# Other job orders on four engines, and other counts of constant products on TensorE, in a fused two-layer transformer kernel

## The reference, cut to what matters

```
x = x + L0_xattn(layernorm(x), ctx)   # 16 heads of width 8, softmax over 77 keys
x = x + L0_ffn(layernorm(x))          # 128 -> 352 -> 128, SiLU gate; activations and weights rounded to
                                      # 8-bit integers with ONE scale, the maximum over the whole tensor
x = x + L1_xattn(layernorm(x), ctx)   # as the first, with a mask
x = x + L1_ffn(layernorm(x))          # 8 experts of 128 -> 256 -> 128, all computed and summed,
                                      # times a normalised top-1 gate
```

## Time and profile before

| | |
|---|---|
| median of 3 runs | 358.16 us (358.93, 352.06, 358.16) |
| the profiled execution | 357.13 us, its span 355.3 us |
| mean granted TensorE clock over the span | 0.897 of 2.4 GHz |
| PE / DVE / ACT / POOL busy | 82% / 73% / 43% / 30% |
| experts, 251 to 351 us | PE busy 98.70 of 100 us |

### The profile page before, as it was taken

One profiled execution on the slowest core, in us unless ns is written; L12 is line 12 of the kernel. 1 busy time (PEld: TensorE's weight loads), 2 busy tenths in 40 slices (PEclk: granted clock), 3 DMA queues, 4 the chain that ended last, 5 costly groups with the idle time before them and its releaser, 6 DMA issues.

```text
span 355.3 us, 4665 instructions
## 1 busy us (share of the span) xinstructions
PE 290.0 (82%) x1368; PEld 180.3 (51%) x1368; DVE 259.4 (73%) x717; ACT 154.3 (43%) x252; POOL 105.0 (30%) x119
## 2 busy tenths in 40 slices
PE   8594887788886363449778989989999999999995
PEld 3262433444444221223455354624678888888883
DVE  4868368878384489883877377772799998898883
ACT  1110255455663175241025355647734554554541
POOL 5785602001001499021108001010136611603400
PEclk9986599999999857696756599999999999999998
DMA  8558131300005900302223121000000000000000
GB/s 153 168 153 202 45 74 22 83 17 2 8 0 95 241 3 0 118 0 63 64 53 72 27 52 44 9 0 9 2 2 0 0 31 1 0 31 0 1 30 30
DMA packets 12298, 16.92 MB, mean 48 GB/s; under 512 B 3672, under 2 KB 6712, under 8 KB 12265
## 3 DMA queue, kind: packets, MB, share of 16 engines
q1 hardware_dynamic: 10018, 11.75, 14.0%
q0 software_dynamic: 1856, 4.27, 4.6%
q10 hardware_dynamic: 400, 0.61, 0.7%
HBM read 4.90 MB, written 1.05 MB: 17 GB/s over the span
## 4 chain that ended last, share of the span: by engine, by line
PE 45%; DVE 16%; ACT 4%; issue 3%; POOL 1%; DMA 1%; SPq 0%; DVEq 0%; POOLq 0%; ACTq 0%
PE ps_acc L1118 4%; PE ps_acc L1117 4%; PE ps_acc L1116 4%; PE ps_tok L986 4%; PE ps_key L995 3%; PE ps_acc L1144 3%; DVE mx L676 3%; PE ps_key L1103 2%; PE ps_key L902 2%; DVE axb L888 2%; PE ps_key L1104 2%; PE ps_key L1105 2%; PE ps_tok L1103 2%; PE ps_tok L1105 2%; PE ps_tok L1104 2%
## 5 line engine op out<-in xcount | busy, mean ns | idle before, releaser
L676 DVE TENSOR_REDUCE mx<-ps_tok 128x4 f32<-128x312 f32 x128 | 57.2, 476 | 23.4 <-PE ps_tok L986 22.1
L467 ACT ACTIVATE big<-ps_key 117x512 f32<-117x512 f32 (+1 forms) x96 | 53.7, 594 | 42.7 <-PE ps_key L995 41.8
L986 PE MATMUL ps_tok<-kst,qst 97*128 97x312 f32 x128 | 50.7, 433 | 17.2 <-DVE mx L676 11.6
L350 POOL TENSOR_SCALAR veps<-mv 128x4 f32<-128x4 f32 x16 | 4.3, 271 | 157.3 <-DVE mv L584 157.2
L986 PEld LDWEIGHTS ps_tok<-kst,qst 97*128 97x128 f32 x128 | 27.5, 219 | 42.3 <-DVE mx L676 20.7
L825 DVE TENSOR_TENSOR qst<-big,qst 128x512 fp32r<-128x512 f32 x64 | 44.3, 692 | 2.2
L995 PE MATMUL ps_key<-qst,kst 105*117 105x512 f32 (+1 forms) x96 | 41.8, 469 | 4.6 <-ACT big L467 3.7
L902 PE MATMUL ps_key<-spin 128*128 128x512 bf16 x109 | 35.0, 469 | 1.4 <-DVE spin L862 1.4
L527 ACT ACTIVATE big<-ps_tok,b 128x512 f32<-128x512 f32 x32 | 21.9, 689 | 22.7 <-PE ps_tok L1105 21.8
L527 ACT ACTIVATE big<-ps_key,b 128x512 f32<-128x512 f32 x32 | 22.1, 689 | 22.5 <-PE ps_key L1105 20.9
L823 DVE CAST qst<-big 128x512 fp32r<-128x512 f32 x64 | 27.0, 422 | 5.4 <-ACT big L527 5.2
(11 more groups left out here) (199 smaller groups left out, 538.6 us busy)
## 6 DMA issues: line engine op xcount, KB each, us to landing
qst<-qhi SPq DMA_DIRECT2D x64, 64.0 KB, 2.0
qst<-qlo SPq DMA_DIRECT2D x32, 64.0 KB, 2.0
w1f<-in_w POOLq DMA_DIRECT2D x2, 1024.0 KB, 7.7
kst<-rbuf SPq DMA_DIRECT2D x12, 156.0 KB, 7.3
kst<-rbuf POOLq DMA_DIRECT2D x12, 117.0 KB, 6.1
x<-in_x SPq DMA_DIRECT2D x4, 256.0 KB, 9.2
out<-xn SPq DMA_DIRECT2D x4, 256.0 KB, 2.0
qst<-mthl SPq DMA_DIRECT2D x32, 16.0 KB
```

What stands on the lines that cost most here:

```text
L467: act.activation(p[0:w, j, :], key[n % 2][0:w, :], ACT.Exp, scale=SCALE).then_inc(q["p_ready"], 1)
L676: nc.vector.tensor_reduce(mx[:, u % 2, t, g, 0, :], tok[n % 2][:, 0:KG].rearrange("p (h j) -> p h j", h=HG), AX.X, ALU.max).then_inc(q["to ...
L986: mm(tok[n % 2][:, 0:KG], qst[0:MASKROW + 1, s, g, 128 * t:128 * t + 128], kst[0:MASKROW + 1, b, g, :], start=True, stop=True).then_inc(q[ ...
```

## The change

Only the strings in `ORDER` for ACT, DVE and PE and the counts in `SPIN` and `IDLE` change. SP's string, POOL's program, all operations, tiles and waits stay. The constant products go from 109 to 105: in layer 0 from 50 to 36 (beside the 15 of `SPIN_FIRST`), in layer 1 from 44 to 54. The diff, cut to the parts that the steps speak of:

```diff
 "ACT" layer 0
-  xt/0 q/0 xt/1 q/1 max/0 key/0/0 xt/2 key/0/1 q/2 key/0/2-9 max/1 key/0/10-11 copy/0 xt/3 ...
-  key/3/1-3 ot/2 key/3/4-11 nt/2 copy/3 ot/3 nt/3
+  xt/0 q/0 xt/1 q/1 max/0 key/0/0 xt/2 key/0/1 q/2 key/0/2-10 max/1 key/0/11 xt/3 copy/0 ...
+  key/3/3 ot/2 key/3/4-7 nt/1 key/3/8-11 nt/2 copy/3 ot/3 nt/3
 "DVE" layer 0
-  lnstat/0 lnx0/0 lnstat/1 q/0 vr0/0 kwide/0 tok/0/0-2 lnx0/1 tok/0/3 vr0/1 vr0/2 tok/0/4-6 q/1 tok/0/7
-  lnstat/2 tok/0/8 lnstat/3 tok/0/9-12 vr0/3 lnx0/2 tok/0/13-15 max/0 tok/1/0-6 q/2 tok/1/7-15 max/1 lnx0/3 ...
-  ln/1 on/2 kt/0 wo/2 vr/0 ln/2 vr/1 vr/2 vr/3 on/3 wo/3 ln/3
+  lnstat/0 lnx0/0 q/0 lnstat/1 lnstat/2 lnstat/3 tok/0/0-1 vr0/0 tok/0/2 kwide/0 tok/0/3 lnx0/1 tok/0/4-7 vr0/1
+  tok/0/8-9 q/1 vr0/2 tok/0/10-11 vr0/3 tok/0/12-13 lnx0/2 tok/0/14-15 max/0 tok/1/0-6 q/2 tok/1/7-15 lnx0/3 max/1 ...
+  ln/1 on/2 kt/0 wo/2 vr/0 vr/1 ln/2 vr/2 on/3 vr/3 wo/3 ln/3
 "DVE" layer 1
-  hround/0 hround/1 down/0 hround/2 lnx/0 down/1 q/0 lnx/1 tok/0/0-1 down/2 tok/0/2-5 q/1 tok/0/6-9 lnx/2
-  tok/0/10-13 hround/3 tok/0/14-15 max/0 down/3 tok/1/0-2 q/2 ...
+  hround/0 hround/1 down/0 hround/2 lnx/0 down/1 q/0 lnx/1 down/2 tok/0/0-3 lnx/2 tok/0/4-7 q/1
+  tok/0/8-12 hround/3 tok/0/13-15 max/0 down/3 tok/1/0-4 q/2 ...
 "PE" layer 0
-  spin0/0 spin0/1 xt/0 spin0/2 spin0/3 vr0/0 q/0 spin0/4 tok/0/0-1 ... xt/1 vr0/3 tok/0/5-6 q/1 tok/0/7
-  spin0/6 spin0/7 tok/0/8-15 max/0 tok/1/0-1 idle/0 xt/2 tok/1/2 key/0/0-1 ...
-  max/1 key/0/11 pv/0/2 tok/2/1 xt/3 tok/2/2 idle/1 key/1/0 ...
-  max/3 wqt/0 wqt/1 pv/2/2 nt/1 idle/3 key/3/0-1 wqt/2 on/2 wqt/3 kt/0 key/3/2-3 ot/2 key/3/4 wo/2 key/3/5-6
-  pv/3/0 key/3/7 vr/0 key/3/8 pv/3/1 key/3/9 vr/1 vr/2 key/3/10 nt/2 key/3/11 pv/3/2 vr/3 on/3 ot/3 wo/3 nt/3
+  xt/0 spin0/0 q/0 vr0/0 spin0/1 vr0/1 spin0/2 spin0/3 tok/0/0-4 ... xt/1 spin0/5 vr0/3 tok/0/8 q/1 tok/0/9-12
+  spin0/6 tok/0/13-15 spin0/7 tok/1/0-1 max/0 idle/0 xt/2 tok/1/2 key/0/0-1 ...
+  max/1 idle/1 key/0/11 xt/3 pv/0/2 key/1/0 ...
+  max/3 key/2/11 wqt/0 wqt/1 pv/2/2 wqt/2 key/3/0 on/2 key/3/1 wqt/3 kt/0 key/3/2-3 ot/2 key/3/4-5 pv/3/0
+  key/3/6-7 wo/2 vr/0 nt/1 vr/1 key/3/8-9 pv/3/1 key/3/10-11 nt/2 pv/3/2 vr/2 on/3 vr/3 ot/3 wo/3 nt/3
 "PE" layer 1
-  spin1/0 down/0 spin1/1 down/1 spin1/2 xt/0 q/0 spin1/3 spin1/4 xt/1 tok/0/0 spin1/5 tok/0/1 q/1 down/2
-  idle/0 tok/0/2-3 ... spin1/9 tok/0/8-15 xt/2 max/0 down/3 q/2 tok/1/0 key/0/0-1 ...
+  spin1/0 down/0 spin1/1 down/1 spin1/2 xt/0 idle/0 q/0 spin1/3 spin1/4 down/2 spin1/5 spin1/6 spin1/7 tok/0/0
+  xt/1 tok/0/1-3 q/1 tok/0/4-11 idle/1 tok/0/12 xt/2 tok/0/13-14 spin1/8 tok/0/15 tok/1/0 max/0 down/3 q/2
+  spin1/9 key/0/0 ...
...
-        SPIN = ((3, 4, 4, 0, 8, 3, 4, 2), (8, 4, 6, 0, 12, 0, 0, 0, 1, 1))
-        IDLE = ((8, 7, 2, 5), (5, 0, 2, 5))
+        SPIN = ((2, 0, 11, 0, 3, 0, 1, 4), (11, 1, 11, 2, 0, 3, 7, 2, 4, 4))
+        IDLE = ((7, 4, 4, 0), (3, 0, 1, 5))
```

## The result

The changed kernel takes 340.24 us (median of 6 runs, 339.07 to 346.25) against 357.11 us (352.06 to 358.93, 6 runs): a ratio of 0.960, 95% interval 0.952 to 0.967. The profiled execution took 339.07 us, the fastest of the six; its span is 337.3 us. The lists of three engines changed (ACT, DVE, PE), not of four as the title has it.

The account below looks back on a forecast made before the run. PE bounds the experts; before them DVE is fairly full, with PE setting the pace at half clock in places. Terms 0 - 0.3 - 1.4 - 3.0 + 0 = -4.7 us on 357.13 give 352.4, taken as 352.9; range 348.5 to 358.5.

Parts of the forecast that it names:

- The start, 0: Layer 0 up to unit 0's first key: earlier queries and the new wait of `max/0` balance; 0, from -0.8 to +1.5 us.
- Unit 1's keys and the middle, -0.3: Layer 0, ahead of `key/1/0`: fewer constant products and earlier `xt/3`, mostly discounted because DVE is nearly full; -0.3 us.
- The end of layer 0, -1.4 of 1.9 us: End of layer 0's attention: last keys ahead of `nt/2`, and its layernorm earlier; 1.4 taken of 1.9 us.
- Both named parts: `key/3/11` ahead of `nt/2`, 1.1 us; `idle/3`'s five products and `nt/1` no longer ahead of `key/3/0`, up to 0.8 us.
- Layer 1's opening, -3.0 us: First `qlo` to unit 4's maxima: `down/2` before the first score fills DVE's idle 4.2 us, less 1.2 us for constant products.
- The rest, 0: `on/3` behind `experts/1`, and single `tok` and `key` jobs trading places: 0, from -1 to +1 us.
- rival 1: Layer 1 behind unit 4's maxima: new constant products bring the clock to full, -4.2 us more, 348.5 us; chance 0.20.
- Rival 2: Freed time is waited out: the opening's gain is lost, layer 0's end keeps 0.7 us; 356.5 us, chance 0.25.
- Rival 3: Layer 0, with 14 constant products fewer, falls to half clock: one unit gives 358 us, two give 364; chance 0.10.

Follow-up runs that it names:

- the front of layer 0 alone: Kernel before with the new lists and counts of layer 0 up to `wqt/0` and `on/2`, the old ones behind: 352.54 us against 357.96, ratio 0.994.
- The run with both sides' moves: Kernel before with `lnx0/3` and `round/1` moved on DVE, `xt/3` and `q/3` earlier on PE and ACT, fewer constant products: 356.01 us against 356.24, ratio 0.995.
- the roundings: Kernel before with two DVE moves: `lnx0/3` ahead of `max/1`, and `round/1` directly behind `round/0`: 358.66 us in its only execution.
- the new counts: Kernel before with all lists old and only the counts of constant products new: 359.38 us against 357.05, ratio 1.004.
- the end alone: Kernel before with new lists only from `wqt/0` (PE, ACT) and `on/2` (DVE) to the end of layer 0's attention, `idle/3` at 0: 355.33 us against 357.96.

## Why the prediction was wrong, step by step

**The start, 0: right.** +0.67 and -0.07 us up to maxima 1; the DMA of unit 1's queries releases its first score at 37.14 us; `max/0` behind it costs nothing that a median shows.

**Unit 1's keys and the middle, -0.3: the first step that failed.** It measured -3.3 us in the profiles (-2.71, -0.63), and the front of layer 0 alone gives 5.4 us by the medians, 2.3 by the ratio. I had found the waits (fewer products, `xt/3` ahead of `pv/0/2`) and then struck them out by the sentence that DVE is nearly full "with the same jobs in sum". Two things were wrong in it. The jobs were not the same in that stretch: `lnx0/3` left it for the one before, where DVE had idle time, worth 1.17 us in the stretch that it left:

```profile
34.60:52.38 17.78, 15.06 (x56) 7.89 (x60) 8.87 (x20) 6.87 (x13) 5.45 (x12) 0.77 0.27 64
```

There (kernel before, maxima 0 to 1) DVE is busy 8.87 of 17.78 us. And DVE was idle for 4.2 of the 20.50 us; with PE's query and transposes earlier, these went to 2.6 (15.21 busy in 17.82). The run with both sides' moves has 18.09 us.

**The end of layer 0, -1.4 of 1.9 us: the mechanism right, the sum short.** It measured -3.16. Both named parts have the sizes that I gave them, 0.98 and 0.80 us, each taken back alone; if they add, which no run tests, cutting 1.9 to 1.4 was unfounded. Of the other 1.4 us, 0.4 came with the front's lists (32.94 with the old end); the rest lies in moves of this part that I left uncosted; which ones, no run shows.

**Layer 1's opening, -3.0 us: mis-sized by the clock.** It measured -4.31, and 0.96 more before it, at the first query. I had taken the old trace's clock for the new kernel: 1.2 us for constant products at half clock delaying the first score, and nothing for the first query, which took 2.08 us. The clock was at full (2.75 us for twelve, 1.13 for the query), so my upper bound of 4.2 us was had. `down/2` is a condition of this and not a gain by itself: alone it is worth nothing by the medians, taken out of the new lists it costs 6.9 us. The 0.96 us is not had every time: with `max/0` ahead and with `key/3/11` back, whose traces have a short fall of the clock near 155 us, that stretch takes 17.4 us.

**The rest, 0: the second step that failed**, though rival 1 named it. Units 5 to 7 measured -6.1 us against the 4.2 of that rival. Beside the trace with `down/2` alone, about 4.4 of them are the clock (17.80 to 15.13 and 19.45 to 17.74), which is that rival's size, and 1.7 are the traded `tok` and `key` jobs (0.3, 0.85 and 0.6), which I had at nothing. By the medians the eight products around `max/0` and `key/0/0` are worth 4.8 us, the eight before the first query 3.9, all 54 together 7.1. I gave this a chance of 0.20 and kept it out of the sum. Its 348.5 us already has the clock on top of the forecast's waits, about 9 us; the other 8 are what the front, the end, the opening, the traded jobs and the experts gave beyond my terms. The experts' 0.78 us I had at nothing: PE went through them in 98.37 instead of 99.15 us. Except for the execution of 651.55 us, every trace with the new lists of layer 1 has this gain, whatever the counts, and none with the old ones has it. `on/3` stands behind two experts' steps instead of one there, but DVE's `wo/3` and `ln/3` moved too, and no run separates them.

**The sum** by the profiles: +0.6, -3.3, -3.2, -1.0, -4.3, -6.1, -0.8 is -18.1 us of span; the medians differ by 16.9, and the profiled execution of the changed kernel was its fastest.

**Rival 2** (waited out) describes what the single moves do: `down/2` alone, unit 2's moves alone and `lnx0/3` alone all shorten their stretch by 1.2 to 2.4 us and leave the time where it was. In the trace of unit 2's moves there is a fall of the clock right behind; for the other two why it is lost stays open. For the whole change it is refuted. **Rival 3** is refuted: layer 0 lost 14 products, and its clock never fell between 42 and 113 us. In fact it is the old lists of the front that had dips between 43 and 113 us: none in the traces of the kernel before and of `lnx0/3` alone, one with `down/2` alone and one with the roundings, two with the new counts and two with PE's moves, four with the end alone; of the eleven traces with the new front one had a dip (new lists with old counts, 93 to 96.5 us). This fits that the front's median gain, 5.4 us, is larger than what its stretches lose against one trace without dips (3.3); that it is the cause is argued, not shown.

**The size of it all.** I summed one trace at the clock that this trace had. In these runs the lists and the constant products together moved where the clock fell and rose, and the clock changed the waits in turn; I counted the waits and left the clock where it was. What makes the clock fall or rise at one place and not at another, the runs do not settle.

## What to carry to other kernels

Where TensorE's clock changes during a kernel, price each moved job at both clocks, and price the wait that it removes twice: once as idle time and once as the half clock behind it; here, in layer 1, the opening gave 5.3 us and the clock in the two stretches behind it about 4.4. A single move can shorten its stretch by 2 us and the kernel by nothing; judge such moves in the full set as well, by taking one out of it, and not only by putting one into the old order. Before you write that an engine is full and its jobs are the same in sum, count its idle time and its jobs between the same two marks in both lists.

## What the hardware showed that I had not expected

Half clock is no sign of an idle TensorE. It stood at 0.50 to 0.52 for 10 and for 14 us with PE busy in all of them, in mixes of scores, keys and values. Behind some strings of the constant bf16 product the clock rose (at 165.7 us before the change, within the twelve from 161.67), but it rose behind such a mix too, at 192.2 us without any constant product. "TensorE: Matmul & The Clock Gate" in the Trainium skill (Part 1: The HAM clock gate) says that activity releases the throttle; in these rows the release came only after 10 and 14 us of it, by what PE's busy time shows.

One execution of six of the kernel with layer 0 old and layer 1 new took 651.55 us. Its windows and one of its groups, beside the same group on the changed kernel's page:

```profile
500.00:600.00 100.00, 100.00 (x182) 61.82 (x181) 34.79 (x81) 19.63 (x29) 13.25 (x6) 1.00 0.01 3
```
```profile
L901 PE MATMUL ps_key<-spin 128*128 128x512 bf16 x119 | 75.5, 827 | 1.4 <-DVE spin L861 1.4
```
```profile
L901 PE MATMUL ps_key<-spin 128*128 128x512 bf16 x98 | 31.2, 464 | 2.3 <-DVE spin L861 1.4
```

TensorE went through 182 instructions in 100 us of the experts, where the kernel before had 460, and the granted clock was still given as 1.00. One expert product started 0.62 us after the last, where it is 0.23 in the changed kernel, and PE was already this busy in the first 100 us (93.08 of 100). The other engines' work kept its length: DVE was busy 265.1 us in all (259.0 in the changed kernel), ACT 159.4 (155.2). The same page of the Trainium skill warns that the clock's record in a trace can be unreliable and that the gate has been seen stuck; what held TensorE back in this execution, no run here shows. No other execution here did this.
